# The digit comparison of the degree count, moved in part to POOL and to whole-group ScalarE passes

## The reference, cut to what matters

```
deg_out = jax.ops.segment_sum(ones_e, src, num_segments=n)
norm_src = jax.lax.rsqrt(jnp.maximum(deg_out, 1.0))
```

## Time and profile before

| | |
|---|---|
| time, median of 3 runs | 9199.41 us (9197.67 to 9201.44) |
| time of the profiled execution | 9199.44 us |
| span of its instructions | 9197.7 us |
| busy: PE, DVE, ACT, POOL | 6739.5, 6439.9, 4907.6, 6445.9 us |
| the stretch from 163.5 to 349 us, busy: L611, L615, L635, L638 | 95.7, 83.2, 129.6, 55.0 us |
| clock granted to PE in that stretch | 0.50 |

### The profile page before, as it was taken

One profiled execution on the slowest core, in us unless ns is written; L12 is line 12 of the kernel. 1 busy time (PEld: TensorE's weight loads), 2 busy tenths in 40 slices (PEclk: granted clock), 3 DMA queues, 4 the chain that ended last, 5 costly groups with the idle time before them and its releaser, 6 DMA issues.

```text
span 9197.7 us, 142619 instructions
## 1 busy us (share of the span) xinstructions
PE 6739.5 (73%) x36545; PEld 5376.9 (58%) x36545; DVE 6439.9 (70%) x18587; ACT 4907.6 (53%) x11025; POOL 6445.9 (70%) x6952
## 2 busy tenths in 40 slices
PE   4444444555579999999989999956666666649998
PEld 3333344444447777788867888745555555536665
DVE  7867666666689999766667777755565555576667
ACT  6777777777787777311138886611111111166665
POOL 0277777777517777777767777767777777747777
PEclk6555565555699999999999999955555555559997
DMA  3222222222377777888877773222222222210001
GB/s 57 48 53 54 53 52 53 52 53 53 79 235 265 262 257 261 308 318 310 320 267 253 259 255 113 67 54 55 55 54 54 55 54 54 55 45 2 2 2 29
DMA packets 496930, 1132.39 MB, mean 123 GB/s; under 512 B 149951, under 2 KB 353155, under 8 KB 476944
## 3 DMA queue, kind: packets, MB, share of 16 engines
q0 software_dynamic: 214224, 496.11, 20.1%
q10 hardware_dynamic: 21456, 488.12, 13.6%
q1 hardware_dynamic: 260464, 139.04, 5.6%
HBM read 879.71 MB, written 249.48 MB: 123 GB/s over the span
## 4 chain that ended last, share of the span: by engine, by line
PE 32%; DVE 17%; POOL 16%; issue 14%; ACT 14%; DMA 4%; DVEq 2%; SPq 1%; ACTq 0%; POOLq 0%
PE banks L1421 10%; PE banks L2273 6%; PE banks L2634 5%; POOL step_data L1454 5%; POOL step_data L1764 4%; ACT banks L1182 4%; POOL arena L2031 4%; POOL gather_ring L1454 3%; DVE keys L1106 3%; PE banks L1046 2%; ACT onehot L1035 2%; DVE keys L1115 2%; ACT onehot L1033 2%; PE banks L2234 2%; PE banks L2225 2%
## 5 line engine op out<-in xcount | busy, mean ns | idle before, releaser
L1021 POOL DMA_INDIRECT gather_ring<-mean_rows,step_data x1660 | 1598.3, 963 | 744.4 <-issue 314.1
L2031 POOL DMA_INDIRECT arena<-attention_rows,step_data x1660 | 1603.7, 966 | 530.8 <-issue 335.5
L1046 PE MATMUL banks<-gather_ring,onehot 128*128 128x130 f32 x3320 | 950.0, 449 | 1129.2 <-DVE arena L1079 951.6
L1421 PE MATMUL banks<-arena 128*128 128x384 bf16 x8232 | 1556.5, 328 | 40.1 <-DMA arena<-split_out 25.1
L1046 PEld LDWEIGHTS banks<-gather_ring,onehot 128*128 128x128 f32 x3320 | 791.7, 300 | 1280.8 <-issue 1034.5
L1421 PE MATMUL banks<-arena,keys 128*128 128x384 bf16 x7938 | 1493.4, 326 | 0.0
L1421 PEld LDWEIGHTS banks<-arena 128*128 128x128 bf16 x8232 | 1135.9, 138 | 278.9 <-issue 45.2
L1421 PEld LDWEIGHTS banks<-arena,keys 128*128 128x128 bf16 x7938 | 1092.3, 138 | 221.2 <-issue 2.2
L1764 POOL DMA_INDIRECT step_data<-next_rows,window_idx x992 | 946.6, 954 | 339.4 <-issue 300.1
L1454 POOL DMA_INDIRECT step_data<-hidden,window_idx x944 | 913.6, 968 | 300.3 <-issue 282.0
L2273 PE MATMUL banks<-arena,onehot 128*128 128x129 f32 x3320 | 948.7, 443 | 2.6 <-DVE arena L2166 2.6
(11 more groups left out here) (379 smaller groups left out, 13584.4 us busy)
## 6 DMA issues: line engine op xcount, KB each, us to landing
arena<-count_rows ACTq DMA_DIRECT2D x48, 3136.0 KB
keys<-count_rows ACTq DMA_DIRECT2D x46, 3136.0 KB
count_rows<-arena ACTq DMA_DIRECT2D x25, 3136.0 KB
count_rows<-keys ACTq DMA_DIRECT2D x24, 3136.0 KB
gather_ring<-mean_rows,step_data POOLq DMA_INDIRECT x1660
arena<-attention_rows,step_data POOLq DMA_INDIRECT x1660
step_data<-next_rows,window_idx POOLq DMA_INDIRECT x992
step_data<-hidden,window_idx POOLq DMA_INDIRECT x944
```

The source lines that it names most:

```text
L1021: e.indirect_dma_start(ring_at(rings.slot(name, i), SUM_COLS, SUMS - 1), None, rows, bass.IndirectOffsetOnAxis(src_idx[:, i:i + 1], 0), bo ...
L1046: e.matmul(pass_bank[i % N_SUM_BANKS][:, 0:SUMS], onehot[:, i % STEP_SLOTS, :], ring_at(rings.slot(name, i), SUM_COLS, SUMS), start=True, ...
L1421: m = e.matmul(pass_bank[n % 2][:, 0:SPLIT_COLS], counts[t % 2][:, :, h], split[:, h, :], start=(h == 0), stop=(h == NODE_TILES - 1))
L2031: e.indirect_dma_start(row_ring[:, row_slot(j), :], None, attention_rows, bass.IndirectOffsetOnAxis(src_idx[:, j:j + 1], 0), bounds_check= ...
```

## The change

From group 56 on the high one-hots of 11 groups in every 20 (0, 2, 4 ... 18 and 19 of each turn of 20) are made in three instructions on two engines: POOL subtracts the column numbers from the digits for all 8 columns at once (`hist_gpsimd`, one `tensor_tensor` of 784 columns with both inputs in SBUF), ACT takes the absolute value of the 784 columns in one activation, and ACT makes 1 - that, cut at zero, as before. The first 56 groups keep two of five and the eight small activations. The high one-hots get separate slots: two for the groups of DVE, five for those of ACT (three in `keys`, two in `onehot`), each reused when the group that had it last is summed.

```diff
+HIST_POOL_FROM, HIST_TURN = 56, 20
+HIGH_VECTOR, HIGH_KEYS, HIGH_HOTS = 2, 3, 2
...
     def far(i):
 
-        return i % 5 in (0, 2)
-
-    FARS = list(itertools.accumulate((far(i) for i in range(HIST_GROUPS)), initial=0))
+        if i < HIST_POOL_FROM:
+            return i % 5 in (0, 2)
+        k = (i - HIST_POOL_FROM) % HIST_TURN
+        return k % 2 == 0 or k == HIST_TURN - 1
...
+    def hist_gpsimd(e):
+        e.wait_ge(prep_vector.sem, mark["digits"])
+        for i in pool_highs:
+            to, free = high_slot(i)
+            e.wait_ge(hist_summed, free)
+            e.tensor_tensor(to, *high_operands(i), ALU.subtract).then_inc(codes_set)
...
             if not far(i):
-                e.tensor_tensor(
-                    high_store[:, s, :, :],
...
+                to, free = high_slot(i)
+                if free:
+                    e.wait_ge(hist_summed, free)
+                e.tensor_tensor(to, *high_operands(i), ALU.is_equal).then_inc(hist_high)
...
-                for c in range(HIST_COLS):
-                    at = i * HIST_COLS + c
-                    e.activation(to[:, c, :], iota_half[0:LOAD_PARTS, 0:NODE_TILES], ACT.Abs, bias=high_digit[:, at:at + 1],
-                                 scale=-1.0).then_inc(hist_far)
-                e.wait_ge(hist_far, HIST_COLS * FARS[i + 1])
+                (to, free), k = high_slot(i), high_place[i]
+                if i >= HIST_POOL_FROM:
+                    e.wait_ge(codes_set, pool_highs.index(i) + 1)
+                    e.activation(to, to, ACT.Abs).then_inc(hist_far)
+                else:
...
+                e.wait_ge(hist_far, FARS[k + 1])
                 e.activation(to, to, ACT.Relu, bias=ones[0:LOAD_PARTS, 0:1], scale=-1.0).then_inc(hist_near)
...
     def gpsimd(e):
         prep_pool_program(e)
+        hist_gpsimd(e)
         e.wait_ge(prep_vector.sem, mark["edges_made", STEP_GROUPS - 1])
```

More of the change, by code:

```diff
@@ L460, in program @@
     steps_back = sem("step_data_back")
-    codes_set = sem("pool_code_iotas")
+    codes_set = sem("pool_digit_distances_and_code_iotas")
     codes_made = sem("vector_code_iotas")
@@ L569, in program @@
                            for i in range(2))
-    high_store = keys[0][0:LOAD_PARTS, 0:HIST_SLOTS * HIST_COLS * NODE_TILES // 2].bitcast(BF16).rearrange(
-        "p (s c w) -> p s c w", s=HIST_SLOTS, c=HIST_COLS)
+    high_words = HIST_COLS * NODE_TILES // 2
+    high_in_keys = keys[0][0:LOAD_PARTS, 0:(HIGH_VECTOR + HIGH_KEYS) * high_words].bitcast(BF16).rearrange(
+        "p (s c w) -> p s c w", s=HIGH_VECTOR + HIGH_KEYS, c=HIST_COLS)
+    high_in_hots = onehot[0:LOAD_PARTS, 1:STEP_SLOTS, :].rearrange("p s e -> p (s e)")[
+        :, 0:HIGH_HOTS * high_words].bitcast(BF16).rearrange("p (s c w) -> p s c w", s=HIGH_HOTS, c=HIST_COLS)
+    high_vector = [high_in_keys[:, s, :, :] for s in range(HIGH_VECTOR)]
+    high_scalar = [high_in_keys[:, HIGH_VECTOR + s, :, :] for s in range(HIGH_KEYS)] + [
+        high_in_hots[:, s, :, :] for s in range(HIGH_HOTS)]
     low_store = keys[0][0:LOAD_PARTS, 2 * LANE // 4:2 * LANE // 4 + HIST_SLOTS * HIST_COLS * P // 2].bitcast(
@@ L599, in far, with high_slot, high_operands @@
     def far(i):
-        return i % 5 in (0, 2)
-    FARS = list(itertools.accumulate((far(i) for i in range(HIST_GROUPS)), initial=0))
+        if i < HIST_POOL_FROM:
+            return i % 5 in (0, 2)
+        k = (i - HIST_POOL_FROM) % HIST_TURN
+        return k % 2 == 0 or k == HIST_TURN - 1
+    vector_highs, scalar_highs = ([i for i in range(HIST_GROUPS) if far(i) == by] for by in (False, True))
+    pool_highs = [i for i in scalar_highs if i >= HIST_POOL_FROM]
+    high_place = {i: k for groups in (vector_highs, scalar_highs) for k, i in enumerate(groups)}
+    FARS = list(itertools.accumulate((1 if i >= HIST_POOL_FROM else HIST_COLS for i in scalar_highs), initial=0))
+    def high_slot(i):
+        groups, store = (scalar_highs, high_scalar) if far(i) else (vector_highs, high_vector)
+        k = high_place[i]
+        return store[k % len(store)], groups[k - len(store)] + 1 if k >= len(store) else 0
+    def high_operands(i):
+        cols = slice(i * HIST_COLS, (i + 1) * HIST_COLS)
+        return (high_half[:, cols].rearrange("p (c o) -> p c o", o=1).to_broadcast([LOAD_PARTS, HIST_COLS, NODE_TILES]),
+                iota_half[0:LOAD_PARTS, 0:NODE_TILES].rearrange("p (o w) -> p o w", o=1).to_broadcast(
+                    [LOAD_PARTS, HIST_COLS, NODE_TILES]))
+    def hist_gpsimd(e):
[4 more added lines that the diff above has]
+            e.tensor_tensor(to, *high_operands(i), ALU.subtract).then_inc(codes_set)
     def hist_vector(e):
@@ L614, in hist_vector @@
             if not far(i):
-                e.tensor_tensor(
-                    high_store[:, s, :, :],
-                    high_half[:, cols].rearrange("p (c o) -> p c o", o=1).to_broadcast([LOAD_PARTS, HIST_COLS, NODE_TILES]),
-                    iota_half[0:LOAD_PARTS, 0:NODE_TILES].rearrange("p (o w) -> p o w", o=1).to_broadcast(
-                        [LOAD_PARTS, HIST_COLS, NODE_TILES]), ALU.is_equal).then_inc(hist_high)
+                to, free = high_slot(i)
+                if free:
+                    e.wait_ge(hist_summed, free)
+                e.tensor_tensor(to, *high_operands(i), ALU.is_equal).then_inc(hist_high)
             yield
@@ L629, in hist_scalar @@
             if far(i):
-                to = high_store[:, i % HIST_SLOTS, :, :]
-                if i >= HIST_SLOTS:
-                    e.wait_ge(hist_summed, i - HIST_SLOTS + 1)
-                for c in range(HIST_COLS):
-                    at = i * HIST_COLS + c
-                    e.activation(to[:, c, :], iota_half[0:LOAD_PARTS, 0:NODE_TILES], ACT.Abs, bias=high_digit[:, at:at + 1],
-                                 scale=-1.0).then_inc(hist_far)
-                e.wait_ge(hist_far, HIST_COLS * FARS[i + 1])
+                (to, free), k = high_slot(i), high_place[i]
[3 more added lines that the diff above has]
+                else:
+                    if free:
+                        e.wait_ge(hist_summed, free)
+                    for c in range(HIST_COLS):
+                        at = i * HIST_COLS + c
+                        e.activation(to[:, c, :], iota_half[0:LOAD_PARTS, 0:NODE_TILES], ACT.Abs,
+                                     bias=high_digit[:, at:at + 1], scale=-1.0).then_inc(hist_far)
+                e.wait_ge(hist_far, FARS[k + 1])
                 e.activation(to, to, ACT.Relu, bias=ones[0:LOAD_PARTS, 0:1], scale=-1.0).then_inc(hist_near)
@@ L647, in hist_tensor @@
             e.wait_ge(hist_low, i + 1)
-            e.wait_ge(hist_near if far(i) else hist_high, FARS[i + 1] if far(i) else i + 1 - FARS[i + 1])
+            e.wait_ge(hist_near if far(i) else hist_high, high_place[i] + 1)
             for c in range(HIST_COLS):
-                m = e.matmul(hist, low_store[:, s, :, c], high_store[:, s, c, :], start=(i == c == 0),
+                m = e.matmul(hist, low_store[:, s, :, c], high_slot(i)[0][:, c, :], start=(i == c == 0),
                              stop=(i * HIST_COLS + c == LOAD_COLS - 1))
@@ L1358, in codes_vector @@
     def codes_vector(e):
-        e.wait_ge(codes_set, 2)
+        e.wait_ge(codes_set, len(pool_highs) + 2)
         e.wait_ge(tile_end, NODE_TILES)
```

## The result

| | before | after |
|---|---|---|
| time, median (range) | 9200.42 us (9197.67 to 9204.64, 4 runs) | 9254.76 us (9249.97 to 9259.59, 4 runs) |
| time and span of the profiled execution | 9199.44 and 9197.7 us | 9255.46 and 9253.7 us |
| first product of the last 147 groups | 164.03 us | 167.49 us |
| end of the last product | 347.99 us | 412.46 us |
| **the stretch** | **184.0 us** | **245.0 us** |

The changed kernel is slower: the ratio is 1.0059 with a 95% interval of 1.0046 to 1.0072, some 54 us (42 to 66). I had forecast 9289 us with 9265 to 9336 as the range. The sign and the cause were right, the size was not: the stretch (the last 147 groups, the row in bold) grew by 61.0 us and not by 83.0.

A forecast was written before the change was run, and what follows sets the result against it. ACT was taken to bound the stretch before, DVE and POOL together after: 147.0 + 75 x 1.60 = 267.0 us against 184.0 (+83.0), plus 6.4 early, so 9199.4 + 89.4 = 9289 us, range 9265 to 9336.

The forecast's parts named there:

- 83.0: Forecast growth in us of the stretch of the last 147 groups, from 184.0 to 267.0 us.
- What bounds before, and that the end of the count sets everything behind it: ACT's 3.12 us a far group bounds the 184.0 us stretch; its gain or loss reaches the time one to one.
- DVE's own time, 147.0 us: In the changed stretch, DVE's 143 low and 65 high one-hots plus 3.3 us alone would allow 147.0 us.
- ACT and PE covered: In the changed stretch, ACT's pairs at 1.84 us total 148.5 us with one old group; PE is covered, 107.6 us busy.
- Two SBUF inputs on each engine take turns: In the stretch DVE and POOL instructions block each other; chance 0.80, nearly all of it in 9265 to 9336 us.
- the rival: No blocking between POOL and DVE in the stretch: ACT binds at 151.5 us, time 9167 us; chance 0.15.
- The charge, 1.60 us a subtraction: DVE time lost to each POOL subtraction: 1.72 - 0.20 = 1.52 us, plus 0.08; times 75 in the stretch.
- duration of 1.72 us: Estimated length of one POOL subtraction of 784 columns: 0.124 us fixed plus 0.846 x 784/415.
- handover of 0.08 us: Added to each subtraction's cost on DVE, because successive DVE instructions overlap by that and a separated pair cannot.
- +89.4: Forecast growth in us of the whole time: +83.0 in the stretch and +6.4 in the edge lookups.
- My lower bound, 1.45: Least DVE cost of a subtraction, 0.77 x 784/415 us with no handover; used for the 9265 us end.
- The four early subtractions, 6.4 us: Subtractions before the stretch, in the edge lookups where DVE sets the pace: 4 x 1.60 = +6.4 us.

The follow-up runs named there:

- old_shares: The changed kernel with two of five groups far all through, so 53 subtractions in the stretch instead of 75; stretch 235.0 us, time 9255.01 us.
- all_numbers_in_psum: The changed kernel with both DVE comparisons reading their column numbers from PSUM in fp32; stretch 221.7 us, time 9258.78 us.
- write_only: The changed kernel with each POOL subtraction replaced by eight memsets, waits and signals kept, output wrong; stretch 147.5 us, time 9149.92 us.
- numbers_in_psum: The changed kernel with only DVE's high comparison reading its column numbers from PSUM in fp32; stretch 216.3 us, time 9223.62 us.
- dense_inputs: The changed kernel with POOL subtracting two plain bf16 rows of 784 columns, nothing repeated, output wrong; stretch 258.1 us, time 9275.93 us.
- fp32_inputs: The changed kernel with POOL subtracting fp32 digits and column numbers, both repeated as before; stretch 245.2 us, time 9255.20 us.
- three_of_eight: The kernel before with three of eight groups far from group 56 on, instead of two of five; stretch 173.9 us, ratio 0.9983.
- pe_differences: Against the kernel before: PE makes the differences of 6 in 20 groups, 3 far the old way, 11 DVE's, POOL none; stretch 160.8 us, ratio 0.9973.
- pe_more: pe_differences with 8 in 20 groups by PE, 2 far the old way, three of five far in the first 56; stretch 157.6 us, ratio 0.9960.

## Why the prediction was wrong in its size and right in its cause

**What bounds before, and that the end of the count sets everything behind it.** Right as far as the end of the first layer, and not quite one to one behind it. The stretch took 184.0 us, with the change 245.0, and 64.5 us appear at `norm_src`, at the first gather, and still at the last addition of the first layer (2547.9 against 2483.5 us). The whole differs by 56.0 us between the profiled executions and by 54 in the medians. 5.0 of the missing 8.5 us lie in the third layer: from the start of the first of POOL's 1660 gathers there to the start of the last it was 2108.2 us before and 2103.2 after. In the nine other runs it was 2104.4 to 2112.7 us, with no relation to the length of the count; it was not shorter in old_shares (2108.2) or all_numbers_in_psum (2108.9). I take this as the spread of executions; that it is nothing else is not shown.

**DVE's own time, 147.0 us.** Right to 0.5 us (write_only).

**ACT and PE covered.** Right. ACT's pair was 1.73 us, not 1.84, and hid in any case.

**Two SBUF inputs on each engine take turns.** Right, and shown for these instructions by four runs: take POOL's reads away and the loss goes (write_only); take DVE's second SBUF input away in one comparison and it is never held up (numbers_in_psum), in both and neither engine feels the other (all_numbers_in_psum); change the number of subtractions and the loss follows at 1.30 us each (old_shares). The type of the inputs is not the cause, as L2360, in fp32, was held up as well. The Trainium skill ("SBUF — State Buffer", Who interferes with whom) says just this of a DVE instruction with two SBUF inputs and a GpSimd instruction that reads SBUF, and that one which only writes does not contend. The runs agree: 685 ns in the median beside memsets, 1289 in the mean beside subtractions. The words "for the whole instruction" stand on that page beside DVE's two-port modes and not beside the case of two inputs, to which I had carried them over. The measured part here is 1.30 of 1.50 us.

Two things stay open. No run gives POOL an instruction with a single SBUF input, so whether one input is enough to hold DVE up is not shown. And L2652, which I counted for the rival, says nothing for sharing: it falls between POOL's instructions. At 9128.49 it ran for 0.26 us, when POOL's instruction from 9127.76 had 0.06 us to go and the next had not begun at 9128.62. In none of the 98 does one of POOL's instructions cover it.

**The charge, 1.60 us a subtraction: the step that failed.** It was mis-sized twice. The duration of 1.72 us came from a row with plain operands; with both operands repeated it is 1.50 (dense_inputs gives 1.68). And the handover of 0.08 us is not there: a held-up pair takes 2.58 us, its usual 1.28 and 1.30 more, and the instruction behind it begins before it ends, as ever (230.10 against 230.18). With 1.50 - 0.20 = 1.30 the same sum gives 147.0 + 75 x 1.30 = 244.5 us, against 245.0. Of my 83.0 us, 75 x 0.22 = 16.5 and 75 x 0.08 = 6.0 were not there. The rest of the distance between +89.4 and the measured +54 is the early subtractions (2.9), what the later layers took less (8.5) and the difference between profiled execution and median (1.7). My lower bound, 1.45, took a proportional length for the least possible; I had written that no row shows a repeated operand, and yet let no bound reach below the plain one.

**The four early subtractions, 6.4 us.** Too much. The timeline of POOL and DVE around three of them, with PE's last product before the weights and, at the end, its first behind them:

```profile
144.79 2.61 DVE L645 TENSOR_TENSOR keys<-arena 125x1024 bf16<-125x1024 bf16 x2
...
145.37 1.49 POOL L637 TENSOR_TENSOR onehot<-arena,iota_half 125x784 bf16<-125x784 bf16 x1 [6.99 <-PE banks L687]
...
152.25 1.50 POOL L637 TENSOR_TENSOR onehot<-arena,iota_half 125x784 bf16<-125x784 bf16 x1 [5.39 <-PE banks L687]
152.42 2.48 DVE L645 TENSOR_TENSOR keys<-arena 125x1024 bf16<-125x1024 bf16 x2
...
155.31 1.83 POOL L637 TENSOR_TENSOR keys<-arena,iota_half 125x784 bf16<-125x784 bf16 x1 [1.56 <-PE banks L687]
155.71 2.58 DVE L645 TENSOR_TENSOR keys<-arena 125x1024 bf16<-125x1024 bf16 x2
...
157.75 0.87 PE L687 MATMUL banks<-keys 125*128 125x98 bf16 x8 [0.97 <-DVE keys L645]
...
167.49 1.51 PE L687 MATMUL banks<-keys 125*128 125x98 bf16 x16
```

The pair of low comparisons at 144.79 took 2.61 us and that at 152.42 2.48, instead of 1.28: together 2.53 us. The third held up the pair at 155.71, the first of which PE's product at 157.75 waited for. Before, that product (at 154.29) waited for ACT, and DVE's one-hot for it had been ready for 1.0 us; so only 0.34 us of the third charge reached PE. The fourth, at 158.70, fell into the time when DVE was ahead and waited for PE anyway. The stretch began 3.5 us later: these 2.53 and 0.34, and 0.61 that was there before the first subtraction (POOL's last lookup of edge rows at 137.38 instead of 136.77).

## What to carry to other kernels

Before work goes from DVE or ACT to an idle POOL, look at what both read: if DVE's neighbours there have two SBUF inputs and POOL's instruction has two as well, count POOL's duration less 0.2 us as DVE time, and expect DVE to gain nothing from a move that saves it less than that (here it paid 1.30 us for 0.89). An engine at 0% is not free capacity if it must take turns with a busy one; the way from PE over PSUM to ACT left DVE's low comparisons at 684 to 702 ns. And take a duration from a row with the same access pattern, or let the bound reach past the row on both sides.

## What was not expected of the hardware

A POOL tensor_tensor of 784 columns is shorter when its operands are repeated by a step of zero: 1.50 us against 1.68 with two plain rows, and the same 1.50 in fp32 and bf16.

The clock granted to PE in the stretch did not follow from the work in it. From 170 to 300 us it was 0.50 (the 1.2 GHz level) in fp32_inputs, where PE was busy for 63.6 of 130 us, and 1.00 (2.4 GHz) in dense_inputs with 60.6 busy; three_of_eight had 1.00 from 60 to 155 us and 0.50 after. In pe_differences and pe_more it was 0.96 and 0.97, with PE busy for 99.5 and 108.8 of the 130 us. As DVE set the pace in fp32_inputs and dense_inputs (from 170 to 300 us it waited 1.6 us for PE in each), the clock can hardly have changed their comparison; whether the two versions with PE's differences would gain as much at 0.50 stays open.
